# Side-job interval 15 to 12 in attention, and re-buffered output stage, in a transformer layer kernel

## The chip, the cores and the metric

The kernel runs on the 8 cores of one Trainium2 chip, one batch element per core, and every core does the same work on its own data. The metric is the device time of the slowest core, in microseconds (us).

## The reference

One layer for x of shape (8, 2048, 2048): layer norm, attention with rotary position code and a causal mask, and beside it a feed-forward part with ternary weights; the result is x plus their product.

```python
xn = _layernorm(x, axis=-1)
s = attention(xn)                       # 32 heads of 64, causal, 2048 positions
def _quantize(w):
    gamma = jnp.mean(jnp.abs(w))
    return jnp.clip(jnp.round(w / (gamma + EPS)), -1.0, 1.0)
x1 = xn @ _quantize(w1).T               # w1, w2: (5632, 2048)
x2 = xn @ _quantize(w2).T
hidden = sigmoid(x1) * x2
g = silu(hidden @ _quantize(w3).T)      # w3: (2048, 5632)
out = x + s * g
```

## The kernel before

The program is written as Python loops that append instructions to five streams (PE, ACT, DVE, POOL, SP); each engine then runs its own stream strictly in order, and waits on semaphores where the code says so. `emit` (line 69) appends a compute instruction, `dma` (line 98) a transfer. Transfers on "sy" are issued by SP, those on "sw" by POOL, those on "sq" by ACT. All transfers go through the one line 99 (plain) or line 97 (transposing).

The stages, in order:

1. Layer norm, transposes of the normalized x, and the sums of the weights' absolute values.
2. Q, K and V projections. Beside them a part of w1 and w2 is quantized (`emit_quant_some`, 90 of 176 jobs).
3. Attention: 32 heads with 20 tasks each, 640 in all. A task is two 128x512 score matmuls (line 806), one exponential of 128x1024 on ACT (line 814), masks on DVE near the diagonal (line 824), and, two tasks later, two matmuls into `psc` (line 846, `emit_ctx`). After tasks 2, 6, 12 and 20 of a head a reciprocal on DVE (line 852) closes a block of 512 queries, and the next block's matmuls wait until `psc` is read out.
4. Output projection, whose result s goes to memory (`s_sc`).
5. Gate and up matmuls (lines 1024, 1036) into `HIDT`, for 1024 positions at a time (two passes, `lb`).
6. Down matmuls (line 1093) of each pass: four blocks `ob2` of 512 columns. A block loads `w3b` (two halves of 2.8 MB, SP), then runs two groups (`ltq` 0 and 1) of 44 x 4 = 176 matmuls each into one of two PSUM buffers `p63`. Each group is followed by an output stage of 8 steps.

**The side jobs.** What is left of the weight work is done inside attention. `job_tick` counts tasks, and each time it has gone 15 further `emit_tail(8)` writes eight jobs into the streams behind the current task. The list of jobs, in order: 86 quantizing jobs of w1 and w2 (load on POOL, sign on ACT at line 426, two operations on DVE, store on POOL), 64 repack jobs (`emit_repack_some`: a transposing load into `rpb` on SP, a store to w1qT or w2qT on POOL, no compute engine), 64 quantizing jobs of w3 (load into the single buffer `w3ch` on POOL, sign on ACT at line 663, two operations on DVE, store on POOL), and 88 repack jobs of w3 (SP and POOL only). That is 302 jobs, so 38 calls. A quantizing job stands in ACT's and DVE's streams behind the exponential and the masks of its task, and in front of those of the next: while it waits for its load, attention waits too. SP's stream also holds the loads of q and k for the next pair of heads (`emit_qk_loads`, one pair per 40 tasks, written one pair ahead).

**The output stage** (in `build_nc`, lines 1103 to 1145), a step j of eight:

```python
t_xl = P.dma("sy", xob[xb_][:, :], x_in..., waits=[t_xob_free[xb_], t_p4_pe])
t_sl = P.dma("sw", sob[xb_][:, :], s_sc..., waits=[t_sob_free[xb_], ...])
# store of step j-1:
t_od = P.dma("sw", po_, oub[pxb][:, :], waits=[pou])
t_g   = act:  gb6 = silu(0.5 * PSUM)           waits t_wlast, t_gb6_free
t_sg6 = dve:  sgf6 = gb6 * sob[xb_]            waits t_g, t_sl, t_sgf6_free
t_ou  = dve:  oub[xb_] = sgf6 + xob[xb_]       waits t_sg6, t_xl, t_oub_free
t_xob_free[xb_] = t_ou
```

The buffers `xob`, `sob` and `oub` are doubled (step j uses number j modulo 2); `gb6` and `sgf6` are single. The loads of x stand in SP's stream in front of the loads of the next block's `w3b`, and after the first pass in front of those of `w12b`.

Of the kernel before, what the change touches and what calls it, by code (L numbers as in the profile page):

```python
# [7 lines left out]
F32 = mybir.dt.float32  # L8
BF16 = mybir.dt.bfloat16
# [132 lines left out]
def build_nc(cfg: Cfg, dbg=False):  # L142
    L, D, H, NH, HD = cfg.L, cfg.D, cfg.H, cfg.NH, cfg.HD
    LT, DT, HT, OC, QB = cfg.LT, cfg.DT, cfg.HT, cfg.OC, cfg.QB
# [32 lines left out]
    P = Prog(nc, es)  # L177
# [4 lines left out]
    def PSUM(n, sh, dt, st):  # L182
# [6 lines left out]
    C_SZ = max(max(2 * DT * 1024 + 2 * (LT * NH * 2) + 2048, P4RC)  # L189
               + 8192 + 4096 + 512,  # L190
               3 * DT * 512 + 2048,
               2 * HT * 512 + 8192)
    A_OFF = TOP - A_SZ
    B_OFF = A_OFF - B_SZ
    C_OFF = B_OFF - C_SZ
# [3 lines left out]
    RC = Region(nc, C_OFF, C_SZ)  # L199
# [259 lines left out]
    for mat in ("q", "k", "v"):  # L459
        for oc in range(OC):  # L460
            wb = ("qkv".index(mat) * OC + oc) % 2
            tws = []
            for dt in range(DT):
# [3 lines left out]
                    waits=[t_wXT_free[wb], t_cast["w" + mat]]  # L467
# [7 lines left out]
                          waits=[t_bias[bsl]])  # L475
            gi0 = "qkv".index(mat) * OC + oc
            t_last_mm = None
            for lt in range(LT):
# [3 lines left out]
                ps = pqkv[myps]  # L482
# [392 lines left out]
    job_tick = 0  # L875
    for gi in range(NT + 2):
        if gi < NT:
            emit_scores_exp_mask(gi)
        if gi >= 2:
            emit_ctx(gi - 2)  # L880
        job_tick += 1
        if job_tick % 15 == 0:
            emit_tail(8)
    t_p4_pe = P.tok("pe")
    t_p4_act = P.tok("act")
# [80 lines left out]
    RC.cur = 0  # L966
    w3b = [RC.take(f"w3b_{i}", [128, HT * 256], BF16) for i in range(2)]
    RC.cur = max(RC.cur, 3 * ((DT * 512 + 63) & ~63) + 2 * 512)
    gb6 = RC.take("gb6", [128, 256], BF16)
    sob = [RC.take("sob0", [128, 256], BF16), RC.take("sob1", [128, 256], BF16)]  # L970
    xob = [RC.take("xob0", [128, 256], F32), RC.take("xob1", [128, 256], F32)]
    oub = [RC.take("oub0", [128, 256], F32), RC.take("oub1", [128, 256], F32)]
    sgf6 = RC.take("sgf6", [128, 256], F32)
    t_w3b_free = [None, None]
    t_p63_free = [None, None]
    pend_ost = [None]
    t_gb6_free = None
    t_xob_free = [None, None]
    t_sob_free = [None, None]
    t_oub_free = [None, None]  # L980
    t_sgf6_free = None
    t_hid_free = t_s_done + [t_p5_dve]
    t_wlast = None
    NHC = H // 256
    for lb in range(LBS):
# [89 lines left out]
        for ob2 in range(D // 512):  # L1075
            tl_h = [None, None]
            for h in range(2):
                in3 = bass.AP(w3qT, ob2 * (H * 512) + h * HT2 * 128 * 512,
                              [[512, 128], [128 * 512, HT2], [1, 512]])
                tl_h[h] = P.dma("sy", w3b[h][:, :], in3,  # L1080
                                waits=[t_w3b_free[h], t_w3T_all[0], t_hid_done,
                                       t_w12_free[0], t_w12_free[1],
                                       t_w12_free[2]])
            for ltq in range(NLB // 4):
                pq = ltq % 2
                ps = p63[pq]
                for h in range(2):
                    for htl in range(HT2):
                        ht = h * HT2 + htl
                        for lt4 in range(4):  # L1090
                            ltl = ltq * 4 + lt4
                            P.emit("pe", (lambda pp, ht_, ltl_, l4, hh, hl:
                                          lambda e: e.matmul(  # L1093
                                pp[:, l4 * 512:(l4 + 1) * 512],
                                HIDT[:, ht_ * 1024 + ltl_ * 128:
                                     ht_ * 1024 + ltl_ * 128 + 128],
                                w3b[hh][:, hl * 512:(hl + 1) * 512],
                                start=(ht_ == 0), stop=(ht_ == HT - 1)))(
                                    ps, ht, ltl, lt4, h, htl),
                                waits=(([tl_h[h], t_p63_free[pq]])  # L1100
                                       if htl == 0 and lt4 == 0 else []),
                                n=(1 if ht == HT - 1 and lt4 == 3 else 0))
                t_wlast = P.tok("pe")
                if ltq == NLB // 4 - 1:
                    t_w3b_free[0] = t_wlast
                    t_w3b_free[1] = t_wlast
                t_g = None
                for lt4 in range(4):
                    ltl = ltq * 4 + lt4
                    lo = lb * LBL + ltl * 128  # L1110
                    for ss in range(2):
                        ob = ob2 * 2 + ss
                        xb_ = (ltl * 2 + ss) % 2
                        t_xl = P.dma("sy", xob[xb_][:, :],
                                     x_in.ap()[lo:lo + 128,
                                               ob * 256:(ob + 1) * 256],
                                     waits=[t_xob_free[xb_], t_p4_pe])
                        t_sl = P.dma("sw", sob[xb_][:, :],
                                     s_sc.ap()[lo:lo + 128,
                                               ob * 256:(ob + 1) * 256],  # L1120
                                     waits=[t_sob_free[xb_], t_s_done,
                                            t_p4_pe])
                        if pend_ost[0] is not None:
                            po_, pou, pxb = pend_ost[0]
                            t_od = P.dma("sw", po_, oub[pxb][:, :], waits=[pou])
                            t_oub_free[pxb] = t_od
                            pend_ost[0] = None
                        t_g = P.emit("act", (lambda pp, l4, s_: lambda e: e.activation(
                            gb6[:, :], pp[:, l4 * 512 + s_ * 256:
                                          l4 * 512 + s_ * 256 + 256], AF.Silu,  # L1130
                            scale=0.5))(ps, lt4, ss), waits=[t_wlast, t_gb6_free])
                        t_sg6 = P.emit("dve", (lambda xb2: lambda e: e.tensor_mul(
                            sgf6[:, :], gb6[:, :], sob[xb2][:, :]))(xb_),
                            waits=[t_g, t_sl, t_sgf6_free])
                        t_gb6_free = t_sg6
                        t_sob_free[xb_] = t_sg6
                        t_ou = P.emit("dve", (lambda xb2: lambda e: e.tensor_add(
                            oub[xb2][:, :], sgf6[:, :], xob[xb2][:, :]))(xb_),
                            waits=[t_sg6, t_xl, t_oub_free[xb_]])
                        t_sgf6_free = t_ou  # L1140
                        t_xob_free[xb_] = t_ou
                        pend_ost[0] = (out_t.ap()[lo:lo + 128,
                                                  ob * 256:(ob + 1) * 256],
                                       t_ou, xb_)
                t_p63_free[pq] = t_g
        t_hid_free = t_wlast
        es6bp.close()
    if pend_ost[0] is not None:
        po_, pou, pxb = pend_ost[0]
        t_od = P.dma("sw", po_, oub[pxb][:, :], waits=[pou])  # L1150
        t_oub_free[pxb] = t_od
        pend_ost[0] = None
    P.emit("po", lambda e: e.nop(), waits=P.qtok("sw") + P.qtok("sq"))

# [80 lines left out]
```

How the kernel before makes its waits and increments, by code:

```python
    def replay(self, stream, eng):  # L111
        hi = {}
        for ws, fn, sem, n in self.items[stream]:
            for (wsem, wcnt) in ws:
                if wcnt > hi.get(wsem, 0):
                    eng.wait_ge(self.sems[wsem], wcnt)
                    hi[wsem] = wcnt
            ins = fn(eng)
            if n > 0:
                ins.then_inc(sem, n)
```

## Time and profile before

| | us |
|---|---|
| timed runs, two | 8006.5 and 8192.91, median 8099.71 |
| the profiled execution's own time | 7984.77 |
| its span, core 2, the slowest (others from 7919.5) | 7982.4 |
| attention, from 2584 to 5554 | 2970 |
| down matmuls of pass 1 and pass 2 | 448 and 444 |

The profile is one execution. The share of busy time is an average over stages with different limits, so the rows are to be read stage by stage. The span begins at the first instruction and ends after the last transfer. A transfer's time "to landing" counts from the start of its issue to the semaphore that tells its end.

### The profile page before, as it was taken

Reading aid. Unit: us, or ns where it says so; the run is one execution under the profiler, and the core shown is the slowest. Engines: PE = TensorE matmul, PEld = TensorE weight load, DVE = VectorE, ACT = ScalarE, POOL = GpSimd, SP = SyncE. Lnnn points to the kernel's source line nnn. Section 1 sums busy time; section 2 is a strip of 40 time slices with the busy share of each in tenths; the row PEclk is TensorE's granted clock in tenths of the full one; section 3 lists DMA queues with packets and bytes.
Section 4 is the critical chain, followed back from the end, with each engine's and each line's share of the span. In section 5 each row is a group of like instructions: output and inputs, shape, how many; then the busy total and the mean of one; then the engine's idle time right before and its main releaser. Section 6 shows DMA issues by size and latency. Waiting matters only on the chain.

```text
span 7982.4 us, 51660 instructions; the slowest of 8 cores (7919.5 to 7982.4 us)
## 1 busy us (share of the span) xinstructions
PE 4275.8 (54%) x15760; PEld 1493.9 (19%) x15760; DVE 2566.0 (32%) x3595; ACT 1369.6 (17%) x1656; POOL 896.4 (11%) x1440
## 2 busy tenths in 40 slices
PE   0011114564553434356222325766989987799966
PEld 0000001221221000001000000111434433344433
DVE  0145545554322444444133333443112211122111
ACT  0000001222101333233122223333001100011000
POOL 0000002443201010111100001100000001100011
PEclk9855556787776555555555555555999998899988
DMA  9755564334323232368622225500232223322232
GB/s 110 126 178 169 169 164 138 84 82 103 88 72 96 71 93 76 92 166 193 159 92 72 77 74 128 136 18 17 60 108 74 74 78 103 102 77 74 78 111 80
DMA packets 738448, 811.41 MB, mean 102 GB/s; under 512 B 507904, under 2 KB 577920, under 8 KB 735104
## 3 DMA queue, kind: packets, MB, share of 16 engines
q0 software_dynamic: 93376, 360.79, 17.3%
q1 hardware_dynamic: 596416, 300.49, 16.0%
q10 hardware_dynamic: 48384, 146.82, 6.1%
q8 instruction: 131, 2.15, 0.1%
q14 instruction: 141, 1.16, 0.1%
HBM read 533.23 MB, written 222.30 MB: 95 GB/s over the span
## 4 chain that ended last, share of the span: by engine, by line
PE 41%; DMA 25%; DVE 18%; issue 6%; SPq 4%; ACT 3%; another core or an unknown queue 1%; POOL 1%; DVEq 0%; ACTq 0%; POOLq 0%
PE p L1093 8%; DMA gch<-w 8%; PE p L1024 8%; PE p L1036 7%; PE psc L846 6%; PE psS L806 4%; DVE rcs L852 4%; SPq L97 4%; DMA w3ch<-w 4%; PE pqkv L486 3%; DMA w1q<-q2c 3%; PE ps L922 3%; DVE q2c L434 3%; DMA w2q<-q2c 2%; DVE gacc L263 2%
## 5 line engine op out<-in xcount | busy, mean ns | idle before, releaser
L846 PE MATMUL psc<-expb,VBUF 128*65 128x512 bf16 x1280 | 675.3, 630 | 915.2 <-DVE expb L824 589.9
L814 ACT ACTIVATE expb<-psS,negm 128x1024 bf16<-128x1024 f32 x640 | 708.5, 1113 | 1181.1 <-PE psS L806 1181.1
L486 PE MATMUL pqkv<-wXT,XNT 128*128 128x512 bf16 x3072 | 760.9, 405 | 110.3 <-ACT qe L498 93.9
L1093 PE MATMUL p<-w3b,HIDT 128*128 128x512 bf16 x2816 | 624.6, 386 | 214.8 <-DMA w3b<-w3qT 214.8
L1024 PE MATMUL p<-XNT,w12b 128*128 128x512 bf16 x2816 | 640.6, 381 | 61.0 <-issue 36.1
L806 PE MATMUL psS<-qtb,ktb 64*128 64x512 bf16 x1280 | 659.2, 617 | 15.1 <-DMA ktb<-k_sc 15.1
L1036 PE MATMUL p<-XNT,w12b 128*128 128x512 bf16 x2816 | 636.5, 379 | 2.1 <-DMA w12b<-w2qT 2.0
L321 PE MATMUL pstr<-id_sb,xcb 128*128 128x128 bf16 x256 | 29.8, 309 | 1018.8 <-DVE xcb L308 1018.8
L852 DVE RECIPROCAL rcs<-psc 1x512 bf16<-1x512 f32 x128 | 429.4, 3355 | 269.1 <-PE psc L846 268.1
L263 DVE TENSOR_REDUCE gacc<-gch 128x1 f32<-128x1024 f32 (+1 forms) x272 | 322.5, 1188 | 460.6 <-DMA gch<-w 459.9
L854 PE MATMUL psbc<-rcs,ones 1*64 1x512 bf16 x128 | 76.9, 601 | 720.3 <-DVE rcs L852 720.3
L1049 DVE TENSOR_SCALAR x2b<-p 128x256 bf16<-128x256 f32 x352 | 149.4, 424 | 968.0 <-PE p L1036 948.6
L824 DVE TENSOR_TENSOR expb<-expb,ut_sb 128x512 bf16<-128x512 bf16 x512 | 216.9, 425 | 633.5 <-ACT expb L814 606.8
L486 PEld LDWEIGHTS pqkv<-wXT,XNT 128*128 128x128 bf16 x3072 | 300.2, 103 | 522.9 <-issue 243.1
L846 PEld LDWEIGHTS psc<-expb,VBUF 128*65 128x65 bf16 x1280 | 119.8, 144 | 1456.3 <-issue 1456.3
L1093 PEld LDWEIGHTS p<-w3b,HIDT 128*128 128x128 bf16 x2816 | 278.7, 99 | 560.7 <-issue 239.3
L426 ACT ACTIVATE q2a<-dch,nthv 128x1024 bf16<-128x1024 f32 x176 | 201.8, 1146 | 939.0 <-DMA dch<-w 619.4
L491 PE MATMUL pqkv<-bias_sl,ones_r 1*128 1x512 bf16 x192 | 75.8, 395 | 526.8 <-DMA bias_sl<-bk 247.0
L1024 PEld LDWEIGHTS p<-XNT,w12b 128*128 128x128 bf16 x2816 | 276.3, 98 | 396.7 <-issue 67.2
L1036 PEld LDWEIGHTS p<-XNT,w12b 128*128 128x128 bf16 x2816 | 275.1, 98 | 335.6 <-issue 5.9
L1046 ACT ACTIVATE sgb<-p 128x256 bf16<-128x256 f32 x352 | 135.2, 384 | 1076.6 <-DVE HIDT L1052 709.5
L429 DVE TENSOR_SCALAR q2c<-dch,nthv 128x1024 bf16<-128x1024 f32 x176 | 132.4, 752 | 556.2 <-DMA w1q<-q2c 296.9
(107 smaller groups left out, 3092.5 us busy)
## 6 DMA issues: line engine op xcount, KB each, us to landing
gch<-w ACTq DMA_DIRECT2D x256, 512.0 KB, 4.6
dch<-w POOLq DMA_DIRECT2D x176, 512.0 KB, 4.5
w3ch<-w POOLq DMA_DIRECT2D x64, 704.0 KB, 5.4
w3b<-w3qT SPq DMA_DIRECT2D x16, 2816.0 KB, 18.1
w1q<-q2c POOLq DMA_DIRECT2D x88, 256.0 KB, 2.4
w2q<-q2c POOLq DMA_DIRECT2D x88, 256.0 KB, 2.3
w1qT<-rpb POOLq DMA_DIRECT2D x32, 704.0 KB, 5.9
w2qT<-rpb POOLq DMA_DIRECT2D x32, 704.0 KB, 6.6
```

The source lines that it names most:

```text
L97: fn = lambda e: e.dma_start(out=out, in_=in_, transpose=True)
L263: t_gred[b] = P.emit("dve", (lambda bb, cc, ww: lambda e: e.tensor_reduce(gacc[:, cc:cc + 1], gch[bb][:, 0:ww], AX.X, ALU.add, apply_absol ...
L434: tq = P.emit("dve", lambda e: e.scalar_tensor_tensor(q2cb[:, 0:QW], q2cb[:, 0:QW], -1.0, q2a[:, 0:QW], ALU.add, ALU.add), waits=[ts1, tb])
L486: P.emit("pe", (lambda pp, dtt, ltt, wbb: lambda e: e.matmul(pp[:, :], XNT[:, dtt * L + ltt * 128:dtt * L + ltt * 128 + 128], wXT[wbb][:, ...
L806: lambda e: e.matmul(ps_[:, jj * 512:(jj + 1) * 512], ktb[hbb][rbb:rbb + 64, ktt * 128:ktt * 128 + 128], qtb[hbb][rbb:rbb + 64, qbb * 512: ...
L814: t_exp = P.emit("act", (lambda ps_, ex_, gl, nn: lambda e: e.activation(ex_[:, 0:gl * 512], ps_[:, 0:gl * 512], AF.Exp, bias=negm[:, nn:n ...
L846: t_cm = P.emit("pe", (lambda vs, ex_, jj, st, sp: lambda e: e.matmul(psc[:, :], vs, ex_[:, jj * 512:(jj + 1) * 512], start=st, stop=sp))( ...
L852: t_rc = P.emit("dve", lambda e: e.reciprocal(rcs[64:65, :], psc[64:65, :]), waits=[t_cm, t_rcs_free])
L922: P.emit("pe", (lambda pp, dtt, ltt, wbb: lambda e: e.matmul(pp[:, :], CTX[:, dtt * L + ltt * 128:dtt * L + ltt * 128 + 128], woT[wbb][:, ...
L1024: lambda e: e.matmul(pp[:, :], w12b[b_][:, dtt * 256 + ht_ * 128:dtt * 256 + ht_ * 128 + 128], XNT2[:, dtt * L + lo_:dtt * L + lo_ + 512], ...
L1036: lambda e: e.matmul(pp[:, :], w12b[b_][:, dtt * 256 + ht_ * 128:dtt * 256 + ht_ * 128 + 128], XNT2[:, dtt * L + lo_:dtt * L + lo_ + 512], ...
L1093: lambda e: e.matmul(pp[:, l4 * 512:(l4 + 1) * 512], HIDT[:, ht_ * 1024 + ltl_ * 128: ht_ * 1024 + ltl_ * 128 + 128], w3b[hh][:, hl * 512: ...
```

## The change

It changes two things. In attention the eight side jobs are written after every 12 tasks, no longer after every 15. In the output stage `gb6` and `sgf6` get two buffers each, and `oub` is gone: the sum is written over the x that was loaded into `xob`, and the store reads it from there. So a load of x into `xob` now waits for the store of two steps earlier (`t_xob_free[pxb] = t_od`), where it waited for the addition of two steps earlier; and the addition no longer waits for a store.

```diff
@@
-               2 * HT * 512 + 8192)
+               2 * HT * 512 + 7680)
@@
-        if job_tick % 15 == 0:
+        if job_tick % 12 == 0:
             emit_tail(8)
@@
-    gb6 = RC.take("gb6", [128, 256], BF16)
+    gb6 = [RC.take("gb60", [128, 256], BF16), RC.take("gb61", [128, 256], BF16)]
@@
-    oub = [RC.take("oub0", [128, 256], F32), RC.take("oub1", [128, 256], F32)]
-    sgf6 = RC.take("sgf6", [128, 256], F32)
+    sgf6 = [RC.take("sgf60", [128, 256], F32), RC.take("sgf61", [128, 256], F32)]
@@
-                            t_od = P.dma("sw", po_, oub[pxb][:, :], waits=[pou])
-                            t_oub_free[pxb] = t_od
+                            t_od = P.dma("sw", po_, xob[pxb][:, :], waits=[pou])
+                            t_xob_free[pxb] = t_od
@@
-                            scale=0.5))(ps, lt4, ss), waits=[t_wlast, t_gb6_free])
+                            scale=0.5))(ps, lt4, ss, xb_),
+                            waits=[t_wlast, t_gb6_free[xb_]])
                         t_sg6 = P.emit("dve", (lambda xb2: lambda e: e.tensor_mul(
-                            sgf6[:, :], gb6[:, :], sob[xb2][:, :]))(xb_),
-                            waits=[t_g, t_sl, t_sgf6_free])
+                            sgf6[xb2][:, :], gb6[xb2][:, :], sob[xb2][:, :]))(xb_),
+                            waits=[t_g, t_sl, t_sgf6_free[xb_]])
@@
                         t_ou = P.emit("dve", (lambda xb2: lambda e: e.tensor_add(
-                            oub[xb2][:, :], sgf6[:, :], xob[xb2][:, :]))(xb_),
-                            waits=[t_sg6, t_xl, t_oub_free[xb_]])
-                        t_sgf6_free = t_ou
-                        t_xob_free[xb_] = t_ou
+                            xob[xb2][:, :], sgf6[xb2][:, :], xob[xb2][:, :]))(xb_),
+                            waits=[t_sg6, t_xl])
+                        t_sgf6_free[xb_] = t_ou
```

The first place is ACT's stream in attention, between two calls of the side jobs in the w3 phase (`expb` are the exponentials of the tasks, `w3qa` the signs of the jobs). The piece is of the difference; around it stand 12 more exponentials that both have.

```order
 L814 ACTIVATE expb_71<-psS,negm 128x1024
 L814 ACTIVATE expb_72<-psS,negm 128x1024
-L814 ACTIVATE expb_70<-psS,negm 128x1024
-L814 ACTIVATE expb_71<-psS,negm 128x1024
-L814 ACTIVATE expb_72<-psS,negm 128x1024
 L663 ACTIVATE w3qa<-w3ch,nthv 128x1408 x8
 L814 ACTIVATE expb_70<-psS,negm 128x1024
```

Three tasks fewer stand between two calls. The first two `w3qa` of all stood 120 exponentials behind the last `q2a` (the sign of a w1 or w2 job); they now stand 96 behind it, and all 38 calls are written by task 456, where it was task 570.

The second place is SP's stream during the repack of w1 (`rpb` is the repack's transposing load, `qtb` and `ktb` are the loads of q and k for a pair of heads). Before:

```order
L97 DMA_TRANSPOSE rpb_73<-w1q 128x2816
L97 DMA_TRANSPOSE rpb_74<-w1q 128x2816
L97 DMA_TRANSPOSE qtb_78<-q_sc 128x2048
L97 DMA_TRANSPOSE ktb_81<-k_sc 128x2048
L97 DMA_TRANSPOSE rpb_73<-w1q 128x2816
```

In the changed kernel, behind the same first 18 repack loads:

```order
L97 DMA_TRANSPOSE rpb_73<-w1q 128x2816
L97 DMA_TRANSPOSE rpb_74<-w1q 128x2816
L97 DMA_TRANSPOSE qtb_80<-q_sc 128x2048
L97 DMA_TRANSPOSE ktb_83<-k_sc 128x2048
L97 DMA_TRANSPOSE rpb_73<-w1q 128x2816
```

It is the load of one pair of heads earlier: the repack loads have moved ahead in task numbers. Three pairs of q and k loads stood among the 64 repack loads of w1 and w2; now two do.

The third place is SP's stream in the output stage, the loads of x of steps 0 to 3 behind the second load of `w3b`, with the semaphores they wait for (S_dve is DVE's, S_sw numbers are those of POOL's transfers). Before:

```order
L99 DMA w3b_103<-w3qT 128x22x512
L99 DMA xob_107<-x 128x256
L99 DMA xob_108<-x 128x256
L99 DMA xob_107<-x 128x256 [waits S_dve]
L99 DMA xob_108<-x 128x256 [waits S_dve]
```

In the changed kernel:

```order
L99 DMA w3b_103<-w3qT 128x22x512
L99 DMA xob_108<-x 128x256
L99 DMA xob_109<-x 128x256
L99 DMA xob_108<-x 128x256 [waits S_sw26]
L99 DMA xob_109<-x 128x256 [waits S_sw28]
```

Nothing has moved here; the wait has changed, from the addition to the landing of the store.

## Rows read from the trace of the kernel before

**Rows 1.** Stretches of the span: PE, PEld, DVE, ACT, POOL busy, PEclk, DMA share, GB/s
```profile
2584.00:3464.00 880.00, 346.83 (x699) 56.50 (x699) 379.13 (x403) 279.28 (x253) 90.19 (x168) 0.50 0.31 83
3464.00:3827.00 363.00, 244.09 (x492) 39.58 (x492) 155.21 (x168) 132.89 (x120) 54.73 (x52) 0.50 0.86 202
3827.00:3940.00 113.00, 5.90 (x12) 0.94 (x12) 0.85 (x2) 0.44 (x1) 15.57 (x15) 0.50 0.82 205
3940.00:4845.00 905.00, 250.22 (x504) 40.57 (x504) 316.08 (x295) 224.07 (x184) 67.75 (x126) 0.50 0.24 78
4845.00:5554.00 709.00, 486.56 (x981) 79.02 (x981) 301.38 (x327) 261.71 (x236) 63.53 (x89) 0.50 0.30 72
```

**Rows 2.** Timeline of ACT in attention, around the repack of w1 and w2
```profile
3463.88 3.11 ACT L814 ACTIVATE expb<-psS,negm 128x1024 bf16<-128x1024 f32 x3
...
3575.83 1.11 ACT L814 ACTIVATE expb<-psS,negm 128x1024 bf16<-128x1024 f32 x1 [6.25 <-PE psS L806]
...
3584.75 1.12 ACT L814 ACTIVATE expb<-psS,negm 128x1024 bf16<-128x1024 f32 x1 [5.04 <-PE psS L806]
...
3636.23 1.11 ACT L814 ACTIVATE expb<-psS,negm 128x1024 bf16<-128x1024 f32 x1 [6.25 <-PE psS L806]
...
3940.20 1.47 ACT L663 ACTIVATE w3qa<-w3ch,nthv 128x1408 bf16<-128x1408 f32 x1 [112.76 <-DMA w3ch<-w]
```

**Rows 3.** Timeline of SP's queue during the repacks
```profile
3475.82 96.55 SPq L97 DMA_TRANSPOSE rpb<-w1q  x16
3572.46 2.98 SPq L97 DMA_TRANSPOSE qtb<-q_sc  x1
3575.49 5.98 SPq L97 DMA_TRANSPOSE ktb<-k_sc  x1
...
3883.49 42.28 SPq L97 DMA_TRANSPOSE rpb<-w2q  x6
...
4850.40 65.25 SPq L97 DMA_TRANSPOSE rpb<-w3q  x18
```

**Rows 4.** Timeline of ACT around one call of eight w3 jobs
```profile
3988.72 1.46 ACT L663 ACTIVATE w3qa<-w3ch,nthv 128x1408 bf16<-128x1408 f32 x1
...
4056.83 2.10 ACT L814 ACTIVATE expb<-psS,negm 128x1024 bf16<-128x1024 f32 x2
...
4105.20 1.46 ACT L663 ACTIVATE w3qa<-w3ch,nthv 128x1408 bf16<-128x1408 f32 x1
```

**Rows 5.** Chain that ended last, pieces around the down matmuls of the passes
```profile
6490.70 77.54 PE p L1093 x352
6584.98 17.49 DMA w3b<-w3qT
...
7767.26 77.55 PE p L1093 x352
...
7860.04 12.80 DMA w3b<-w3qT
7873.09 77.54 PE p L1093 x352
```

**Rows 6.** Timeline of the last output stage, from 7950 on
```profile
7952.06 0.42 DVE L1137 TENSOR_TENSOR oub<-sgf,xob 128x256 f32<-128x256 f32 x1 [0.24 <-DVE sgf L1132]
...
7953.06 0.54 POOL L99 DMA_DIRECT2D out<-oub  x1 [18.91 <-DVE sgf L1132]
...
7958.06 0.42 DVE L1137 TENSOR_TENSOR oub<-sgf,xob 128x256 f32<-128x256 f32 x1 [0.24 <-DVE sgf L1132]
...
7971.00 0.55 POOL L99 DMA_DIRECT2D out<-oub  x1 [0.87 <-DVE oub L1137]
```

**Rows 7.** Transfers by line: count, KB each, median us to landing
```profile
xob<-x SPq DMA_DIRECT2D x128, 128.0 KB, 3.0
out<-oub POOLq DMA_DIRECT2D x128, 128.0 KB, 3.0
sob<-s_sc POOLq DMA_DIRECT2D x128, 64.0 KB, 3.3
```

More of the change, by code:

```diff
@@ L976, in build_nc @@
     pend_ost = [None]
-    t_gb6_free = None
+    t_gb6_free = [None, None]
     t_xob_free = [None, None]
     t_sob_free = [None, None]
-    t_oub_free = [None, None]
-    t_sgf6_free = None
+    t_sgf6_free = [None, None]
     t_hid_free = t_s_done + [t_p5_dve]
@@ L1124, in build_nc @@
                             po_, pou, pxb = pend_ost[0]
-                            t_od = P.dma("sw", po_, oub[pxb][:, :], waits=[pou])
-                            t_oub_free[pxb] = t_od
+                            t_od = P.dma("sw", po_, xob[pxb][:, :], waits=[pou])
+                            t_xob_free[pxb] = t_od
                             pend_ost[0] = None
-                        t_g = P.emit("act", (lambda pp, l4, s_: lambda e: e.activation(
-                            gb6[:, :], pp[:, l4 * 512 + s_ * 256:
+                        t_g = P.emit("act", (lambda pp, l4, s_, g_: lambda e:
+                                             e.activation(
+                            gb6[g_][:, :], pp[:, l4 * 512 + s_ * 256:
                                           l4 * 512 + s_ * 256 + 256], AF.Silu,
-                            scale=0.5))(ps, lt4, ss), waits=[t_wlast, t_gb6_free])
+                            scale=0.5))(ps, lt4, ss, xb_),
+                            waits=[t_wlast, t_gb6_free[xb_]])
                         t_sg6 = P.emit("dve", (lambda xb2: lambda e: e.tensor_mul(
-                            sgf6[:, :], gb6[:, :], sob[xb2][:, :]))(xb_),
-                            waits=[t_g, t_sl, t_sgf6_free])
-                        t_gb6_free = t_sg6
+                            sgf6[xb2][:, :], gb6[xb2][:, :], sob[xb2][:, :]))(xb_),
+                            waits=[t_g, t_sl, t_sgf6_free[xb_]])
+                        t_gb6_free[xb_] = t_sg6
                         t_sob_free[xb_] = t_sg6
                         t_ou = P.emit("dve", (lambda xb2: lambda e: e.tensor_add(
-                            oub[xb2][:, :], sgf6[:, :], xob[xb2][:, :]))(xb_),
-                            waits=[t_sg6, t_xl, t_oub_free[xb_]])
-                        t_sgf6_free = t_ou
-                        t_xob_free[xb_] = t_ou
+                            xob[xb2][:, :], sgf6[xb2][:, :], xob[xb2][:, :]))(xb_),
+                            waits=[t_sg6, t_xl])
+                        t_sgf6_free[xb_] = t_ou
                         pend_ost[0] = (out_t.ap()[lo:lo + 128,
@@ L1149, in build_nc @@
         po_, pou, pxb = pend_ost[0]
-        t_od = P.dma("sw", po_, oub[pxb][:, :], waits=[pou])
-        t_oub_free[pxb] = t_od
+        t_od = P.dma("sw", po_, xob[pxb][:, :], waits=[pou])
+        t_xob_free[pxb] = t_od
         pend_ost[0] = None
```

## The prediction

> **What bounds the kernel now.** I first cut the span into stretches. In all of attention TensorE's granted clock is 0.50, the lower of its two levels (1.2 GHz), and PE is busy 39% of 880 us in the stretch with w1 and w2 quantizing jobs, 67% of 363 us during the repack, almost not at all for the next 113 us, 28% of 905 us with the w3 quantizing jobs, and 69% of 709 us after them [rows 1]. So attention has two speeds: its own, and a slow one in which it waits for side jobs. Then I read ACT's timeline, since quantizing jobs and exponentials share that engine. Undisturbed, the same pattern of a head comes back from 3575.83 to 3636.23: 60.4 us for 20 tasks, 3.02 us a task, of which each reciprocal's gap is about 5 us [rows 2]. A call of eight w3 jobs holds ACT from 3988.7 to 4056.8, 68 us, and the next call begins at 4105.2 [rows 4]. 15 tasks and one call make the cycle. Between calls nothing of a quantizing job is left in flight that would run beside the tasks, so the cost of those calls is their number times their length, whatever the distance between them.
>
> The repack is different: it uses SP, POOL and transfers alone, so it runs beside the tasks. SP issued its loads from 3475.8 to 3925.8 (3883.49 plus 42.28) without a gap of its own, 62 of the 64 [rows 3]: 7.26 us a job, a chain of load, store and buffer. ACT ran the 120 tasks written beside it from 3463.9 on, came to the first `w3qa` and was idle 112.8 us until 3940.2, because the load of `w3ch` stands in POOL's stream behind the last repack store [rows 2]. The work beside the repack is shorter than the repack; the rest is that hole.
>
> Last I read the output stages. In the chain that ended last, each block of 352 down matmuls is followed by a hole before the `w3b` loads are even issued. First block: matmuls end at 6568.2, loads at 6585.0, 16.7 us. Last such hole: 7844.8 to 7860.0, 15.2 us [rows 5]. There are seven (six before `w3b`, one before `w12b`), 16.0 us in the mean. What fills them: SP's stream holds the x loads of all eight steps in front of the weight loads, and the one of step 7 waits for the addition of step 5. Behind the last block the stage runs alone: matmuls end at 7950.6, the last store is issued at 7971.0, 20.4 us [rows 5, 6].
>
> **Part 1: every 12 tasks.** The 302 jobs still need 38 calls, so the calls that hold ACT and DVE (10 and a part with w1 and w2 jobs, 8 with w3 jobs) keep their number and length: 0. What changes is the cover of the repack. From the last `q2a` to the first `w3qa` stand 96 tasks instead of 120. The chain of 64 jobs doesn't shorten, except that two instead of three pairs of q and k loads stand in it. Such a pair took 9.0 us (3572.46 to 3581.47) [rows 3], the other two somewhat less; I take 8.
> - cover lost: 24 x 3.02 = 72.5 us
> - chain shorter: -8 us
> - hole: 112.8 + 64.5 = 177 us, so +64.5 us.
>
> The check is that before, 120 tasks by this rate are 362.4 us, and ACT shows 363.5 (3940.2 less 112.76 less 3463.9) [rows 2].
>
> Bounds: if less attention beside it let the repack run faster, the gain is at most what the chain's own speed allows. The first 16 loads took 96.55 us, 6.0 each [rows 3]; at that rate throughout, 64 jobs would be 80 us shorter, and part 1 would be -16 us. I see no reason for it, since the chain's later loads were slow with the same attention beside them. The upper bound keeps the three pairs: +72.5 us.
>
> The w3 repack also has 24% less cover, 11 calls over 399 us instead of 498. Its loads go at 3.6 us (65.25 for 18) [rows 3], so 88 take 319 us: still covered. Nobody waits for its end in attention; only q and k loads stand behind it, and they are needed 40 tasks (121 us) apart with at most 32 jobs (116 us) between them. So 0. After it attention runs undisturbed to its end, at the rate it has in the last stretch of rows 1 anyway.
>
> The calls fall elsewhere in the heads: before at four places of 20, now at five, of which two are the very task whose `emit_ctx` starts a reciprocal. A call there could hide the 5 us gap of it, or its DVE operations could queue behind the reciprocal and push the call back as much. With some 19 such calls and two places in five, that is 38 us at most to either side [rows 2]; as the two effects cancel I take 0.
>
> **Part 2: the output stage.** The second `gb6` and `sgf6` let the silu of the next step start early. In the timeline DVE is held up by neither for more than a quarter of a microsecond after step 0, so this hides behind the transfers: at most -1 us a stage. The new wait costs. Before, a pair of steps took 6.00 us from addition to addition (7952.06 to 7958.06) [rows 6]: addition 0.4, store issued 0.5 later, its own slot of 0.5, then the `sob` load 3.3, and the multiplication. The x load ran beside it. Now the x load starts only when the store has landed: addition 0.4, store issue 0.6 later, store landing 3.0, x landing 3.0 [rows 7], then 0.1, and the next addition: 7.2 us a pair. The `sob` load, issued right behind the store, is there before.
>
> Behind the end of the matmuls (0), with the first addition ending at 1.9 as now: store 0 at 2.4, landed 5.4; x of step 2 landed 8.5, added 9.0; store 2 at 9.6, store 3 at 10.8, landed 13.8; x of step 5 landed 16.9, added 17.4; store 5 at 18.0, landed 21.0; then SP may issue the x load of step 7 and, 0.4 later, `w3b` at 21.5. Before it was 16.0. That is +5.5 us, seven times, 38.5 us. At the end of the program the last x load lands at 24.1, the last store goes out at 25.2 instead of 20.4: +4.8. The first stage of every block lies under the 38.9 us of the second group of matmuls (77.54 / 2), needs about 27 now, and costs nothing. Together +43 us.
>
> Bounds: the `sob` load alone sets the pace if stores and x loads land in 2.3 us, and then the stage costs about +2 us, 16 in all; if POOL or the transfers are late by 1 us in each of two rounds more, it is +10 us, 80 in all.
>
> Here the Trainium skill has two rules. DMA: Bandwidth & Descriptors, Anatomy of one DMA, gives a transfer issued by POOL about 2.0 us plus bytes over 436 GB/s, that is 2.3 us for 128 KB (an estimate by that page); the rows have 3.0 for both [rows 7], and the sum by the page's figure would be 16 us smaller. GPSIMD Engine Reference, Specifications, says that GpSimd's SBUF interfaces are shared with VectorE and contend with DVE instructions that have two SBUF inputs. Both additions and multiplications here have two, and the trace agrees at least once: the store at 7953.06 is put down to the end of the multiplication, not to its own addition [rows 6]. It came 0.6 us after that addition's end, and the pace above includes that.
>
> **The sum.** 64.5 + 43 = 107.5 us. The profiled execution took 7984.8 us, so it would be 8092 us. The two timed runs of before were 8006.5 and 8192.9, with a median of 8099.7; the profiled execution lies 22 us under the lower one. I put the forecast on the level between it and that lower run, 7996 us: 8104 us. That is 1.3% slower. About 2%, 160 us, is what a measurement of this kernel can tell from no change.
>
> **Rivals.**
> A. The store and load round trip is much longer than 6 us in the stages beside the weight loads, because transfers of 128 KB queue behind 2.8 MB ones (17.5 us to landing [rows 5]). If a pair took 11 us instead of 7.2, the two and a half rounds to step 7 cost 9.5 us more, 76 us in eight stages: 8180 us, and with the level of before 2.3% slower. It decides from a pair of 9.8 us on ((160 - 107.5) / 8 stages / 2.5 rounds = 2.6 us more than 7.2). Against it: the medians of 3.0 are over all 128 transfers, and the weight loads are issued only after the loads that matter.
> B. The repack keeps its hole at 112.8 us, because fewer tasks beside it let it go at 6.0 us a job. Then only part 2 is left: 7996 + 43 = 8039 us. For it: its first jobs went at 6.0; against it: those ran beside as much attention as the rest.
> C. The calls hide reciprocal gaps (38 us), and the added buffers help more than the x wait costs: part 1 at +27, part 2 at -8: 8015 us, or with B also, under 7950 us. Against it: the chain shows transfers, not silu, between the steps.
>
> **How the numbers follow.** Forecast 60%, A 14%, B 16%, C 10%. The low end takes C's first case, near 8015, and the high end takes A with both terms at their upper bounds (72.5 + 80 + 76 = 229 us, 8225) and some of the distance between the two timed runs of before: 8015 to 8250. Slower by over 2% comes from A, and from the forecast with both terms near their upper bound (152 us) and calls that lengthen: 16%. Faster by over 2% would need more than all of C: 3%. Within 2%: 81%.
>
> **What would show it.** In the changed kernel's trace: ACT's idle time before the first `w3qa` is 170 to 185 us, with 96 exponentials in 290 us ahead of it; calls of eight w3 jobs still 68 to 72 us; SP's queue waits for POOL's transfers in the output stage, and the time from the last matmul of a block to the issue of `w3b` is 21 to 22 us. The prediction is wrong if the hole stays near 113 us, if SP's wait before `w3b` stays at 16 us, or if ACT is held longer or shorter per call.

## The result, and the profile after

| | before | changed |
|---|---|---|
| timed runs | 8183.7 us median of 10 | 8226.2 us median of 11 |
| ratio | | 1.0123, 95% interval 1.0086 to 1.0159 |
| profiled execution, own time | 7984.8 us | 8062.7 us |
| median span of cores 0-3 / 4-7 | 7950.5 / 7952.1 us | 8032.9 / 8040.8 us |

The kernel became 1.2% slower. Single runs of one and the same kernel scatter more than that (the ten of before from 7977 to 8477 us), so only the ratio and the profiles decide between kernels; the ratio leaves out executions in which one half of the chip ran slower at a lower granted clock, and so isn't that of the two medians.

The profile after is of core 1. First the stretches of attention, cut as in [rows 1] at the last `q2a`, at the last exponential in front of the hole, at the first `w3qa` and at the end of the quantizing calls (PE, PEld, DVE, ACT, POOL busy, PEclk, DMA share, GB/s).

```profile
2588.00:3364.00 776.00, 276.84 (x558) 45.20 (x558) 337.97 (x359) 244.70 (x221) 90.73 (x170) 0.50 0.32 93
3364.00:3649.00 285.00, 195.95 (x395) 31.80 (x395) 121.68 (x134) 104.72 (x94) 42.85 (x41) 0.50 0.85 200
3649.00:3843.00 194.00, 5.51 (x11) 0.87 (x11) 4.23 (x4) 0.04 (x1) 26.52 (x26) 0.50 0.78 197
3843.00:4677.00 834.00, 202.26 (x408) 32.89 (x409) 287.40 (x265) 200.96 (x164) 68.09 (x127) 0.50 0.27 85
4677.00:5625.00 948.00, 653.24 (x1317) 106.22 (x1315) 402.03 (x436) 348.52 (x313) 62.91 (x89) 0.50 0.24 56
```

The stretch beside the repack shrank from 363 to 285 us, the empty one after it grew from 113 to 194 us, and together they are as long as they were (476 and 479). The transfers work at the same rate in both stretches (200 and 197 GB/s; before 202 and 205 [rows 1]), with attention beside them or not. TensorE's granted clock is 0.50 in all of it, as before.

ACT's timeline says who was waited for:

```profile
3356.97 1.15 ACT L426 ACTIVATE q2a<-dch,nthv 128x1024 bf16<-128x1024 f32 x1 [5.06 <-DMA dch<-w]
...
3842.95 1.47 ACT L663 ACTIVATE w3qa<-w3ch,nthv 128x1408 bf16<-128x1408 f32 x1 [194.37 <-DMA w3ch<-w]
```

The line of the hole is the one of [rows 2], with 194.4 for 112.8. SP's queue is the one of [rows 3], with 22 repack loads in a row at its end where 6 were:

```profile
3370.74 108.99 SPq L97 DMA_TRANSPOSE rpb<-w1q  x16
3479.82 4.20 SPq L97 DMA_TRANSPOSE qtb<-q_sc  x1
3484.06 2.50 SPq L97 DMA_TRANSPOSE ktb<-k_sc  x1
...
3665.84 163.06 SPq L97 DMA_TRANSPOSE rpb<-w2q  x22
```

Both profiles have this pattern on all eight cores, but not the same sizes (the hole is 83 to 117 us before and 148 to 207 us after). So I took every number from the timelines of all eight cores and give means. A call's length is from its first sign on ACT to the next exponential. The hole before a weight load is from the last matmul of a block to the issue of that load; the gap of PE is from that matmul to PE's next one, so it holds the load's landing too.

| mean of eight cores, us | before | changed | difference |
|---|---|---|---|
| attention, first to last exponential | 2948.7 | 3003.8 | +55.1 |
| the hole before the first `w3qa` | 107.5 | 177.0 | +69.5 |
| calls with w1 and w2 jobs, sum | 391.8 | 407.3 | +15.5 |
| calls with w3 jobs, sum | 563.3 | 569.7 | +6.4 |
| tasks outside calls and hole | 1886.1 | 1849.8 | -36.3 |
| last `q2a` to first `w3qa` | 471.9 | 468.9 | -3.0 |
| last matmul of a block to the weight load, mean of 7 | 15.5 | 19.5 | +4.0 |
| PE's gaps there, sum of 7 | 199.3 | 223.1 | +23.8 |
| last matmul of all to the last store | 20.4 | 21.9 | +1.5 |
| span | 7952.0 | 8033.3 | +81.2 |

The holes before the weight loads grew by 7 x 4.0 = 28 us, but PE's gaps by 23.8 us only: the weight loads are issued later and land a little sooner (16.3 us in the median for 16.9). 55.1 + 23.8 + 1.5 = 80.4 us of the 81.2 by which the mean span grew. Single stages move by a few us between executions: attention with the same code took 2948.7, 2943.6 and 2932.6 us in three profiles with calls every 15 tasks.

One such hole, in the chain that ended last in the changed kernel: the matmuls end at 6627.89, the load is issued 19.8 us later.

```profile
6549.70 78.19 PE p L1091 x352
...
6647.69 12.90 DMA w3b<-w3qT
```

The last output stage of the changed kernel, a pair of steps:

```profile
8028.55 0.43 DVE L1137 TENSOR_TENSOR xob<-sgf,xob 128x256 f32<-128x256 f32 x1 [0.17 <-DVE sgf L1132]
...
8029.55 0.54 POOL L99 DMA_DIRECT2D out<-xob  x1 [17.21 <-DVE sgf L1132]
...
8031.84 14.02 SPq L99 DMA_DIRECT2D xob<-x  x6
...
8034.76 0.42 DVE L1137 TENSOR_TENSOR xob<-sgf,xob 128x256 f32<-128x256 f32 x1 [1.60 <-DMA xob<-x]
...
8041.05 0.43 DVE L1137 TENSOR_TENSOR xob<-sgf,xob 128x256 f32<-128x256 f32 x1 [1.72 <-DMA xob<-x]
```

The addition of the first step of a pair now waits for the x load (`<-DMA xob<-x`), where in [rows 6] it followed the multiplication at once. The x load is issued at 8031.84, 2.3 us after the store at 8029.55: it waits for its landing, as SP's queue shows (whom SP waited for; us in total, times, longest):

```profile
SPq L116 <- DMA out<-xob: 735.4, 115, 43.5
```

The pair takes 6.2 and 6.3 us, not the 7.2 of the prediction. Most of this total wait of 735 us is harmless waiting for a block's matmuls to end.

### The profile page after: what moved, and what is told of

Same layout as the page of the kernel before. It is cut to its first block, busy times and chain, and to the rows that moved or that the text cites. A ratio compares the mean times of both kernels' runs of the same rounds, so it can differ in the third digit from the quotient of the medians.

```text
span 8060.5 us, 51408 instructions; the slowest of 8 cores (7985.5 to 8060.5 us)
## 1 busy us (share of the span) xinstructions
PE 4271.5 (53%) x15760; PEld 1493.0 (19%) x15760; DVE 2560.5 (32%) x3595; ACT 1368.5 (17%) x1656; POOL 893.9 (11%) x1440
## 3 DMA queue, kind: packets, MB, share of 16 engines
q1 hardware_dynamic: 596416, 300.49, 15.5%
## 4 chain that ended last, share of the span: by engine, by line
PE 41%; DMA 26%; DVE 18%; issue 6%; SPq 4%; ACT 3%; another core or an unknown queue 1%; POOL 1%; DVEq 0%; ACTq 0%; POOLq 0%
DMA gch<-w 8%; PE p L1091 8%; PE p L1022 7%; PE p L1034 7%; PE psc L846 6%; PE psS L806 5%; DVE rcs L852 5%; DMA w3ch<-w 4%; SPq L97 4%; PE pqkv L486 3%; DMA w1q<-q2c 3%; PE ps L922 3%; DVE q2c L434 2%; DMA w2q<-q2c 2%; DVE gacc L263 2%
## 5 line engine op out<-in xcount | busy, mean ns | idle before, releaser
L1022 PEld LDWEIGHTS p<-XNT,w12b 128*128 128x128 bf16 x2816 | 276.3, 98 | 391.8 <-issue 62.5
```

The source lines that it names most:

```text
L1022: lambda e: e.matmul(pp[:, :], w12b[b_][:, dtt * 256 + ht_ * 128:dtt * 256 + ht_ * 128 + 128], XNT2[:, dtt * L + lo_:dtt * L + lo_ + 512], ...
```

## The experiments

Ratios are against the kernel before, run on the same chip.

### The interval alone, and the output stage alone

```diff
-        if job_tick % 15 == 0:
+        if job_tick % 12 == 0:
```

> The interval alone: eight jobs after every 12 tasks, output stage as before. Theory 1 (lost cover): the repack is a chain of its own speed, 24 tasks fewer stand beside it, so ACT's idle time before the first w3qa is 170 to 195 us as in the changed kernel (before 113); the calls that hold ACT are 20 to 25 us longer in sum (before 397 + 563 us) and the tasks between them 35 to 40 us shorter; attention is 60 to 70 us longer, the holes before the weight loads of the down matmuls stay at 16 us. Time +0.7 to +0.9% against before. Rival (the time comes from the output stage): hole as before, attention equal, time within 0.2%.

The interval alone: 1.0105, interval 1.001 to 1.0201. The row of ACT on the slowest core, 2:

```profile
3833.17 1.47 ACT L663 ACTIVATE w3qa<-w3ch,nthv 128x1408 bf16<-128x1408 f32 x1 [198.82 <-DMA w3ch<-w]
```

In the mean of the cores the hole is 173.5 us, the calls 405.7 and 574.4, the tasks outside 1850.4, attention 3003.9, and the seven holes before the weight loads 15.3 us. Attention is the changed kernel's (3003.8 us; that they agree to 0.1 us is chance), the output stage is that of before. The hole's mean is as expected, single cores have 142 to 199 us. Attention grew by 55 us in the mean, less than the 60 to 70 expected.

The second kernel is the changed one with `% 15`.

> The output stage alone (in-place sum, x load behind the store, double gb6 and sgf6), eight jobs after every 15 tasks. Theory 1: attention as before (about 2960 us on the slowest core, hole near 113 us), the seven holes before the weight loads 19 us each instead of 16, the last store 21.9 us behind the last matmul instead of 20.4: 7 x 3.1 + 1.5 = 23 us, +0.3%. Rival (as the prediction had it): 21.5 us per hole and 25.2 at the end, 43 us, +0.54%. Second rival (the added buffers pay for the wait): within 0.1%.

The output stage alone: 0.9996, interval 0.9937 to 1.0054. The interval holds all three expectations, so time doesn't decide here, and neither does the mean span (7955.1 us, 7952.0 before): in that execution the stages up to the end of attention were 15 us shorter. The profile of the stage itself does. Attention 2943.6 us, hole 111.7, and the holes before the weight loads 19.2 us in the mean of the cores (15.5 before), the last store 21.5 us behind the last matmul. That is 3.7 x 7 + 1.1 = 27 us, nearest to theory 1's 23; PE's gaps grew by 19.8 us, so some 21 us of it are time. The 5.5 us of the prediction were too many, though the core with the longest has holes of 21.0.

So the two parts add up: the interval makes some 55 us, the output stage 20 to 25. The time of each alone is shown for the interval only.

### oub kept, gb6 and sgf6 doubled

Against the changed kernel, with calls every 15 tasks again:

```diff
+    oub = [RC.take("oub0", [128, 256], F32), RC.take("oub1", [128, 256], F32)]
...
-                            xob[xb2][:, :], sgf6[xb2][:, :], xob[xb2][:, :]))(xb_),
-                            waits=[t_sg6, t_xl])
+                            oub[xb2][:, :], sgf6[xb2][:, :], xob[xb2][:, :]))(xb_),
+                            waits=[t_sg6, t_xl, t_oub_free[xb_]])
+                        t_xob_free[xb_] = t_ou
```

> Two buffers each for gb6 and sgf6, but oub kept with its two buffers, so that the x load waits for the addition as before; eight jobs after every 15 tasks. Theory 1: only the wait of the x load made the holes longer, so they are 15 to 16 us here, and the median landing times of x, out and s are 3.0, 3.0 and 3.3 us as before, because the x load again runs beside the other two. Rival: the shorter landing times of the changed kernel (2.4, 2.3, 2.8) come from the double gb6 and sgf6 or the place of the buffers; then they stay short here and the holes shrink to 13 us.

Its three timed runs (8148 to 8307 us) give no ratio, so only the profile speaks. The holes are 14.8 us in the mean of the cores, 0.2 to 0.7 less than in the runs with the output stage of before (15.0 to 15.5): more than that the doubled `gb6` and `sgf6` don't bring by themselves. So the in-place sum alone costs 19.2 - 14.8 = 4.4 us of hole a stage, 3.5 us of PE's gap. The median landing times differ between cores, so one core is compared with itself, core 0. Before:

```profile
xob<-x SPq DMA_DIRECT2D x128, 128.0 KB, 3.1
out<-oub POOLq DMA_DIRECT2D x128, 128.0 KB, 3.0
```

The changed kernel:

```profile
xob<-x SPq DMA_DIRECT2D x128, 128.0 KB, 2.7
out<-xob POOLq DMA_DIRECT2D x128, 128.0 KB, 2.3
```

`oub` kept:

```profile
xob<-x SPq DMA_DIRECT2D x128, 128.0 KB, 3.1
out<-oub POOLq DMA_DIRECT2D x128, 128.0 KB, 3.0
```

With the in-place sum the store lands in 2.3 us, without it in 3.0. The rival falls: the double buffers of `gb6` and `sgf6` leave the landing times as they were. The 3.0 is not what one x load beside the store costs. Away from the weight loads, on the even cores before, stores issued with one x load in flight landed in 2.5 us in the median, those with two x loads and an s load in 3.1. In the last kernel below most x loads again run beside a store (94 of 128 on core 0, for 30% of their time or more), and both still land in 2.3 and 2.5 us.

### Every 10 tasks, and every 16

```diff
-        if job_tick % 15 == 0:
+        if job_tick % 10 == 0:
```

> Eight jobs after every 10 tasks, output stage as before. Theory 1 (lost cover): 80 tasks, 242 us, stand beside the repack instead of 120, so the hole is 113 + 40 x 3.02 = 234 us less a pair of q and k loads (8) plus what the chain was slower in the changed kernel (17): 225 to 245 us. The calls fall at places 9 and 19 of a head's 20 tasks, none on a reciprocal: calls of w1 and w2 jobs 35 to 36 us each, calls of w3 jobs 68 to 72, tasks outside them 1885 us again; attention 3070 to 3090 us on the slowest core, 110 to 130 more than before. Rival (calls lengthen when they stand closer, from transfers still under way): calls of 40 us and more at every place, attention over 3130 us.

Attention is 3081.0 us in the mean of the cores, 132 more than before, and 3113.5 on the slowest, 25 to 30 more than expected. The hole is 222.4 us in the mean; its one timed run took 8111.1 us. On the slowest core:

```profile
3786.32 1.47 ACT L663 ACTIVATE w3qa<-w3ch,nthv 128x1408 bf16<-128x1408 f32 x1 [257.51 <-DMA w3ch<-w]
```

Last `q2a` to first `w3qa` takes 466.8 us in the mean, with 80 tasks beside the repack as with 96 (468.9) and 120 (471.9). The calls are 389.7 and 557.6 us in sum, shorter than with 15. So the rival (closer calls get longer) falls. What I missed is the tasks outside: 1911 us, not 1885; why, is open.

> Eight jobs after every 16 tasks, nothing else changed against before. Theory 1 (lost cover, now gained): 128 tasks stand beside the repack, 387 us of a chain of some 477 us, so the hole before the first w3qa is 85 to 95 us (before 113). Places: 16 t - 1 modulo 20 is 15, 11, 7, 3, 19, so the calls of w1 and w2 jobs with numbers 3, 4, 8 and 9 fall on a reciprocal and take 40 to 41 us where the others take 35 to 38 (with 12 it was 2, 4, 7 and 9); tasks outside the calls take about 1850 us in sum instead of 1886. Attention 2915 to 2935 us instead of 2959, time -0.3 to -0.5%. Rival (a call's length is from how close the calls stand): all calls at 35 to 37 us, tasks outside 1886 us, attention within 15 us of 2935.

With 16, the hole is 96.4 us in the mean of the cores (expected 85 to 95), attention 2924.0 (25 less than before), the calls with w1 and w2 jobs 402 to 409 us in sum (before 388 to 397), tasks outside 1851.4. On its slowest core, 5, attention took 2961 us, as last `q2a` to first `w3qa` took 514 us there; that core is outside the expectation, the mean inside. The time is unclear (8156.2 us median of 6 with 8095.9 for before, no ratio with an interval), so this run supports the theory by its timeline alone. The third and the fourth call, on core 5:

```profile
2807.75 1.14 ACT L426 ACTIVATE q2a<-dch,nthv 128x1024 bf16<-128x1024 f32 x1
2848.75 3.10 ACT L814 ACTIVATE expb<-psS,negm 128x1024 bf16<-128x1024 f32 x3
...
2887.76 1.14 ACT L426 ACTIVATE q2a<-dch,nthv 128x1024 bf16<-128x1024 f32 x1
2928.24 3.10 ACT L814 ACTIVATE expb<-psS,negm 128x1024 bf16<-128x1024 f32 x3
```

They take 41.0 and 40.5 us; the first and second took 35.7 and 36.7. In the changed kernel the long ones are numbers 2, 4, 7 and 9 of the first ten, the calls written behind a task whose `emit_ctx` starts a reciprocal. What happens in them is seen in the second call of the changed kernel, whose first sign starts at 2692.86:

```profile
2692.85 3.35 DVE L852 RECIPROCAL rcs<-psc 1x512 bf16<-1x512 f32 x1 [3.24 <-PE psc L846]
2696.35 0.60 PE L854 MATMUL psbc<-rcs,ones 1*64 1x512 bf16 x1 [3.61 <-DVE rcs L852]
2697.12 0.68 DVE L858 CAST bcs<-psbc 64x512 bf16<-64x512 f32 x1 [0.92 <-PE psbc L854]
2697.91 0.68 DVE L863 TENSOR_TENSOR CTX<-psc,bcs 64x512 bf16<-64x512 f32 x1
2698.63 0.76 DVE L429 TENSOR_SCALAR q2c<-dch,nthv 128x1024 bf16<-128x1024 f32 x1
```

DVE's part of the first job stands behind the whole chain of the reciprocal, 5.8 us, and the call starts that much later for DVE. In return nobody waits for that chain outside the call. The place of the calls decides both, and not the distance: 12 and 16 have the same five places and the same 1850 us of tasks outside, 15 has 1886, 10 has 1911.

The eight-core means call by call say how much comes back. Between before and changed, the seven calls that moved onto a reciprocal and hold ACT for more than two jobs are 31.4 us longer together, 4.5 each, against the 36.3 us that the tasks outside lost. One call goes the other way, the eighth: 42.7 us before (43.6 and 41.0 in the two other profiles of this attention code), though on no reciprocal, and 35.4 in the changed kernel. What made it long wasn't found.

### The order of the side jobs

Here the 64 quantizing jobs of w3 are written in front of the 64 repack jobs, so that no load that ACT needs stands behind a repack store. Every 15 tasks:

```diff
+            elif w3_i < n_w3q:
+                n0 = w3_i
+                emit_w3_some(min(left, n_w3q - w3_i))
+                left -= w3_i - n0
             elif rp_i < len(repack_jobs):
```

> Only the order of the side jobs is changed: the 64 w3 quantizing jobs stand in front of the 64 repack jobs of w1 and w2, calls after every 15 tasks, output stage as before. Theory 1 (the hole is w3ch's load standing in POOL's stream behind the repack's stores, and the repack being longer than the tasks beside it): the hole before the first w3qa goes (under 10 us), calls of w3 jobs stay at 68 to 72 us, the repacks of w1, w2 and w3 (some 480 and 320 us) lie under the last 355 tasks (1072 us); attention about 2845 us instead of 2959, time -1.3 to -1.5%. Rival (the transfers are the limit, and the hole only moves): PE waits for late q and k loads behind the repack loads on SP's queue, attention 2900 us and more, time within -0.8%.

0.9878, interval 0.9789 to 0.9967 (expected -1.3 to -1.5%), with attention 2848.2 us in the mean of the cores (expected 2845). The row of the first `w3qa` on core 6, from ACT's timeline:

```profile
3441.22 1.47 ACT L664 ACTIVATE w3qa<-w3ch,nthv 128x1408 bf16<-128x1408 f32 x1 [11.30 <-DMA w3ch<-w]
```

And PE's wait for k loads there, from the waits (us in total, times, longest):

```profile
PE psS L811 <- DMA ktb<-k_sc: 17.6, 1, 17.6
```

The hole was removed and did not come back elsewhere: the 17.6 us is the first load of attention, 15.1 us before. The 11.3 us (expected under 10) is a wait within a call, which here passes from the last w1 and w2 jobs to the first w3 jobs. The same with calls every 12 tasks:

> The same order (w3 quantizing in front of the repack), with calls after every 12 tasks. Theory 1: with no engine waiting for the repack, the shorter interval no longer costs the 24 tasks of cover; what can be late is only the q and k loads, of which the repack jobs now leave about 480 us of work in SP's queue for 96 tasks (290 us), with one pair of heads (121 us) of slack: at most 60 to 70 us of waiting by PE for ktb, once. Attention 2845 to 2910 us. Rival (the interval costs by itself, through the length of the calls or the transfers): attention 65 us over the run with 15 and no wait for ktb.

0.9913, interval 0.988 to 0.9945. The ratios with 15 and with 12 don't differ beyond their intervals, the timelines do: attention is 2896.5 us in the mean, 48 more than with 15, with k loads late on every core. The longest wait is on core 1:

```profile
PE psS L811 <- DMA ktb<-k_sc: 92.7, 3, 54.4
```

Less the first load that is 73.8 us there, in two waits; core 0 has the shortest, 21.8 us, and the mean is 52 us. Theory 1 had one such wait of 60 to 70 us at most. It holds in kind, and the 52 us account for the 48; the rival's "no wait for ktb" doesn't hold. The calls became 37 us longer in sum (417 + 581 against 398 + 564). That is the reciprocals again: the eight calls that moved onto one are 40 us longer together, 5 us each, and the tasks outside, less the waits for k, are 40 us shorter. So in this order the places of the calls cost and bring nothing.

### The weight loads in front of the x loads, and four buffers

The w3b loads of the next block are written in front of step 2's x load of the last group; the rest as the kernel with the new order and 15:

```diff
+                        if (ltq == NLB // 4 - 1 and lt4 == 1 and ss == 0
+                                and ob2 + 1 < D // 512):
+                            tl_next = load_w3b(ob2 + 1, t_wlast)
```

> The order of side jobs as in e4_order15 (every 15 tasks), output stage with its buffers as before, but the two w3b loads of the next block are written in front of the x load of step 2 of the last group, so that they wait only for the matmuls. Theory 1 (SP's in-order queue, with x loads in front of the weight loads, makes the holes): six of seven holes shrink from 16 us to under 2 us, 6 x 14 = 84 us, -1.05% beside e4_order15; the x loads of steps 2 to 7 come later behind the 2.8 MB loads, which hides under the next block's matmuls. Rival (the hole is needed by the transfers: the weight loads then share the queue with x, s and out and land as much later): w3b 20 to 30 us to landing instead of 17 to 18, PE's idle time before the blocks falls by under 30 us in all.

0.9761, interval 0.9666 to 0.9856, 1.2% below the kernel with the new order and 15 (0.9761 / 0.9878; the two intervals overlap). PE's wait for w3b over the run on the slowest core of each (us, times, longest), with the new order only:

```profile
PE p L1098 <- DMA w3b<-w3qT: 210.4, 8, 34.4
```

With the weight loads in front of the x loads:

```profile
PE p L1103 <- DMA w3b<-w3qT: 102.9, 8, 13.4
```

These are two different cores. In the mean of all eight, PE's seven gaps fell from 198.1 to 102.8 us in sum, 95 us (expected 84), and w3b's loads land in 16.3 us in the median instead of 17.0. The six holes before `w3b` are 0.1 us, the one before `w12b` stays at 15.4. The rival, that the transfers would take back what the queue gives, falls. The last kernel adds the changed kernel's in-place sum, with four buffers for `xob` and `sob`, and has the weight loads in front of step 4's x load; the memory was there once `oub` was gone and `sgf6` single again.

> e4_order15's order of the side jobs, the hoisted w3b loads (in front of the x load of step 4), and the changed kernel's in-place sum with four buffers each for xob and sob, two for gb6, one for sgf6; calls after every 15 tasks. Theory 1 (the in-place sum costs only because a buffer is needed again two steps later): with four buffers the x load waits for the store of four steps earlier, so the last output stage ends earlier than before (last store 14 to 17 us behind the last matmul instead of 20.4) and the hole before w12b shrinks to 8 to 12 us; against e7_hoist -10 us, against before -2.5%. Rival (the transfers' number sets the pace): last store at 20 us or later.

> The kernel of e9_all once more, for a ratio with an interval: w3 quantizing in front of the repack, hoisted w3b loads, four buffers each for xob and sob. From the spans of e9_all (7753.8 us against 7982.4) -2.7 to -3.0%, attention 2850 us, one hole of 11 to 12 us before w12b. Rival (e9_all's profile was a lucky execution): -2.0% or less.

The first of the two runs took 7755.8 to 8080.0 us in its six executions (spans up to 7753.8 us in the profile) and has no ratio with an interval. The second gave 0.9704, interval 0.9643 to 0.9766: 3% faster than before and 4% faster than the changed kernel by the two ratios. The hole before w12b is 11.4 us, as expected; the last store is 18.4 us behind the last matmul in the mean of the cores, where I expected 14 to 17. Stores two steps apart near the end, on core 4:

```profile
7763.24 0.54 POOL L99 DMA_DIRECT2D out<-xob  x1 [2.37 <-DVE xob L1150]
...
7767.81 0.54 POOL L99 DMA_DIRECT2D out<-xob  x1 [2.26 <-DVE xob L1150]
```

A pair still takes 4.6 us. My reading is that the s load of a step stands behind an earlier step's store in POOL's stream, whatever buffers there are. The timeline of core 0 fits: addition, 0.6 us, issue of the store, 0.5 us, the s load with its 2.3 us to landing, multiplication, addition. It wasn't tried by itself. Whether the in-place sum with four buffers adds anything to e7's kernel can't be told from the intervals, which overlap.

## Why the prediction was right or wrong

**The number.** The forecast of 8104 us came from 107.5 us on top of a level of 7996 us. The 107.5 us, 1.3%, stand against a measured 1.23%, and 81 us in the mean span of the eight cores. The step that failed is the level: I took the lower of two runs and the profiled execution as what a run takes. The median of the two was 8099.7, and against that number 8104 reads as no change, where the kernel became 1.2% slower. With more runs the median of before was 8183.7 and of after 8226.2. A forecast should have put its own 107.5 us on the median that was shown: 8207 us. 8104 is near the low runs of the changed kernel (8068, 8091, 8096 and 8101 us), as 7996 was near the low ones of before (7977, 7990 and 8007 us); that the sum came within 0.1% of the measured ratio is in part luck, since its terms were off in both directions.

**Cover lost, 72.5 us.** Right. Last `q2a` to first `w3qa`, less the hole, was 364.4 us before and is 291.9 us in the mean of the cores: 72.5. With 10 and 16 it is 244.4 and 383.2 us, for 80 and 128 tasks: 3.0 us a task in all four, and the kernel with the other order shows that it is this chain that is waited for.

**The chain shorter by 8 us.** Not settled: 3 us in the mean of the cores, but the chain took 470.3 to 476.2 us in three profiles of the same code with 15, and 465.5 and 468.9 in two with 12. The pair of q and k loads took 6.7 us here (3479.82 to 3486.56). The transfers move 200 GB/s with or without attention beside them, so a queue slot saved may be used by nobody; no run shows that by itself. Rival B ends here: with less attention beside it the repack got no faster.

**The calls' places, 0.** Right in the mechanism: both effects that I named exist, and they nearly cancel (31.4 us longer calls against 36.3 us outside; with the new order 40 against 40). The sum over all calls is still -14.4 us (calls +21.9, tasks outside -36.3), half of it from the eighth call, which was 7.4 us shorter for a reason that isn't known.

**The w3 repack, 0.** Right: no wait for ktb came up. (11 calls over 399 us instead of 498 are 20% less cover, not 24.)

**The output stage, +5.5 us seven times and +4.8.** The mechanism was right, the term mis-sized: +4.0 and +1.5, together 29.5 us for 43, of which 25 us are time on PE. What had the wrong size is "store landing 3.0, x landing 3.0". Those medians were of transfers issued close together, and once they take turns the store lands in 2.3 us (2.2 to 2.5 on all cores) and x in 2.4 to 2.8. The page DMA: Bandwidth & Descriptors of the Trainium skill, Anatomy of one DMA, gives a transfer issued by POOL 2.0 us plus bytes over 436 GB/s, by that page an estimate of 2.3 us for 128 KB. The trace agrees for a store with no x or s load in flight at its issue (2.2 us), and not for one with two x loads and an s load in flight (3.1 us on the even cores, 2.8 on the odd). The sum by that page of the Trainium skill, 16 us smaller, would have been 27 us, nearer than mine. Rival A (11 us a pair) and rival C's gain from the added buffers didn't come; the latter measured 0.7 us a stage at most.

The prediction also took the store at 7953.06, 0.6 us behind its addition, for a sign that VectorE's two-input operations hold GpSimd up. It is none: in the kernel before, 1000 of the 1024 stores of the eight cores start 0.57 to 0.59 us after their addition, 402 of them with an operation of VectorE in between and 598 without. The end of the multiplication only fell close by.

Measured less forecast, the errors have different signs: +5 (hole), -14 (calls and tasks outside), -18 (output, as time on PE), together -27 on a forecast of 107.5.

## What to carry to other kernels

When background jobs on a slow queue run beside compute, ask what a job of the compute engines will find in front of it in that queue: the time is the longer of the two lanes, and squeezing the jobs together only takes cover away. Putting the jobs that hold engines first and those that are transfers only last removed the hole, 100 us of attention, with the same work. Loads that gate the next block belong in front of small loads that don't, and an in-place result needs enough buffers that the next load doesn't meet the store. A forecast of a difference belongs on the median of the runs that are shown, not on their lowest.

## What the runs showed that I had not expected

- Landing times depend on how much is in flight: a 128 KB store lands in 2.2 us alone, in 2.5 with one x load in flight at its issue, in 3.1 with two and an s load (medians of the even cores).
- The cores differ in one execution of one kernel: the hole was 83 us on core 1 and 117 us on core 3 before, and the even cores had x landing in 3.0 to 3.1 us where the odd ones had 2.5 to 2.6. Tasks outside the calls vary by less than 4 us between cores. The slowest core need not be the one with the slowest repack chain (before core 2 with 477 us, where core 4 had 481; after core 1 with 486, where core 6 had 499), so a difference of a few tens of us needs all eight.
